# A gather of features is issued only when the third one ahead of it has landed

## What is computed

```
w_m = (efeat @ W_msg + b_msg).reshape(E, in_f, -1)
w_a = (efeat @ W_attn + b_attn).reshape(E, in_f, -1)
h_src = feat[src][:, :, None]
e1 = w_m * h_src
e2 = w_a * h_src
seg_max = jax.ops.segment_max(e2, dst, num_segments=N)
ex = jnp.exp(e2 - seg_max[dst])
denom = jax.ops.segment_sum(ex, dst, num_segments=N)
attn = ex / denom[dst]
ft = jax.ops.segment_sum(e1 * attn, dst, num_segments=N)
return ft.sum(axis=1)
...
x = _layernorm(x + _L0_gnn_ref(x, edge_attr_16, L0_gnn_W_msg, L0_gnn_b_msg, L0_gnn_W_attn, L0_gnn_b_attn, src, dst), axis=-1)
x = _layernorm(x + _L1_gnn_ref(x, edge_index, edge_attr_16), axis=-1)
```

## Time and profile before

| | |
|---|---|
| median of 3 runs | 2309.12 us (2309.01 to 2309.82) |
| the profiled execution | 2309.43 us |
| its span in the trace | 2307.6 us |
| POOL busy | 1682.1 us (73%), 1748 instructions |
| DVE busy | 1867.7 us (81%), 2922 instructions |
| PE busy | 2005.4 us (87%), 6784 instructions |
| ACT busy | 1306.8 us (57%), 1241 instructions |
| mean share of the 16 DMA engines by the gathers' queue | 9.3% |

### The profile page before, as it was taken

The page is one execution under the profiler, slowest core; times in us unless marked ns, Lnnn a source line. Parts: engine busy times, 40 slices in busy tenths (PEclk is TensorE's granted clock), DMA queues, the critical chain, the costliest instruction groups (busy, mean ns, idle before and its releaser), DMA issues.

```text
span 2307.6 us, 21909 instructions
## 1 busy us (share of the span) xinstructions
PE 2005.4 (87%) x6784; PEld 911.8 (40%) x6784; DVE 1867.7 (81%) x2922; ACT 1306.8 (57%) x1241; POOL 1682.1 (73%) x1748
## 2 busy tenths in 40 slices
PE   2548889998999998899989898899989898998886
PEld 0313334443444444444444443344444443444432
DVE  5557777987888988888987887798878887888886
ACT  6425545655566556665655755565556565565552
POOL 5777777777777777777777777777777777777740
PEclk8758999999999999999999999999999999999998
DMA  6100011001100001000100110101001010110110
GB/s 232 55 13 13 13 15 19 7 13 18 13 12 13 13 13 17 12 12 13 17 12 12 17 12 12 17 12 16 12 12 16 12 15 12 15 15 11 14 27 9
DMA packets 60072, 46.93 MB, mean 20 GB/s; under 512 B 28526, under 2 KB 55679, under 8 KB 59436
## 3 DMA queue, kind: packets, MB, share of 16 engines
q0 software_dynamic: 57776, 29.87, 9.3%
q1 hardware_dynamic: 2172, 15.58, 1.9%
HBM read 44.01 MB, written 1.23 MB: 20 GB/s over the span
## 4 chain that ended last, share of the span: by engine, by line
PE 36%; POOL 30%; issue 14%; DVE 14%; DMA 2%; ACT 2%; POOLq 0%; DVEq 0%; SPq 0%; ACTq 0%
POOL AR L624 29%; PE PX L1048 28%; PE PW L1034 7%; DVE AR L1348 7%; DVE AR L1361 3%; PE PTB L1023 2%; DVE AR L1378 1%; DMA AR<-in_xt,AR 1%; POOL AR L642 1%; DVE AR L1365 1%; POOL y_d L657 1%; DMA AR<-in_dst,QI 1%; ACT PX L881 0%; DVE AR L1379 0%; DMA AR<-in_es,AR 0%
## 5 line engine op out<-in xcount | busy, mean ns | idle before, releaser
L624 POOL DMA_INDIRECT AR<-in_xt,AR x1628 | 1572.2, 966 | 501.0 <-issue 486.6
L1048 PE MATMUL PX<-AR,CS 128*128 128x512 f32 x3304 | 1583.4, 604 | 6.8 <-ACT AR L825 6.6
L1348 DVE CUSTOM_DVE_ANT_1 AR<-PW,AR 128x1024 f32<-128x1024 f32 x826 | 987.7, 1220 | 183.0 <-PE PW L1034 127.6
L1048 PEld LDWEIGHTS PX<-AR,CS 128*128 128x128 f32 x3304 | 633.7, 193 | 586.5 <-issue 462.6
L1034 PE MATMUL PW<-WS,LT 100*128 100x512 bf16 x1652 | 514.8, 398 | 204.0 <-DVE AR L1348 203.0
L1361 DVE TENSOR_TENSOR AR<-AR,PX 128x1024 f32<-128x1024 f32 (+1 forms) x448 | 508.2, 1134 | 74.3 <-ACT PX L881 47.7
L819 ACT ACTIVATE LT<-PTB 100x1024 bf16<-100x1024 bf16 (+1 forms) x224 | 214.3, 957 | 529.8 <-PE PTB L1023 529.8
L883 ACT ACTIVATE AR<-AR 128x2048 f32<-128x2048 f32 (+1 forms) x224 | 429.3, 1917 | 7.3
L887 ACT ACTIVATE PX<-AR 128x1024 f32<-128x1024 f32 (+1 forms) x224 | 217.2, 970 | 326.4 <-DVE AR L1361 323.6
L1034 PEld LDWEIGHTS PW<-WS,LT 100*128 100x128 bf16 x1652 | 144.9, 99 | 584.2 <-issue 290.0
L881 ACT ACTIVATE PX<-AR 128x1024 f32<-128x1024 f32 (+1 forms) x224 | 235.6, 1052 | 22.9 <-DVE AR L1361 21.3
(11 more groups left out here) (149 smaller groups left out, 481.8 us busy)
## 6 DMA issues: line engine op xcount, KB each, us to landing
AR<-in_xt,AR POOLq DMA_INDIRECT x1631, 2.3
AR<-in_ea SPq DMA_DIRECT2D x3, 3128.0 KB, 13.6
AR<-in_ea SPq DMA_DIRECT2D x1, 3120.0 KB, 10.2
AR<-in_es,AR POOLq DMA_INDIRECT x49, 3.5
y_d<-AR POOLq DMA_INDIRECT x49, 2.1
AR<-y_d SPq DMA_DIRECT2D x1, 784.0 KB, 4.6
CS<-in_cst SPq DMA_DIRECT2D x1, 442.0 KB, 5.1
AR<-in_xt SPq DMA_DIRECT2D x1, 392.0 KB, 3.1
```

Source lines behind the costliest of these rows:

```text
L624: g.indirect_dma_start(feat(h, j - j0, j - j0 + 1), None, xt, bass.IndirectOffsetOnAxis(ap=XE[:, at:at + 1], axis=0)).then_inc(hg_sem(h), 16)
L1048: i = pe.matmul(PDR, IDN, x, start=(a == 0 and j == 0), stop=(g == LAST[k] and j == n - 1))
L1348: v.tensor_tensor_reduce(em(g, j, j + 2).rearrange("p (x c) -> p x c", c=32), w, hb, 1.0, LOW, ALU.mult, ALU.max, accum_out=MXC[:, k % 2, ...
```

## The change

Three semaphores `d_h[0..2]` take the place of all those for the gathers. All 1,628 gathers are numbered in the order of issue, x = 0, 1, 2, ..., and gather x adds to `d_h[x % 3]`. From x = 3 on, its issue waits for `d_h[x % 3]` to reach 16 * (x // 3), that is for gather x - 3 to have landed. Who needs a group g waits for all three semaphores, each at the count that it has once the last gather of g and all before it have landed (`landed`). Neither the order of the instructions nor any size is changed. In the changed file the lines of POOL are 1 or 2 lower, L624 is L623 there, and DVE's L1334 is L1330.

```diff
+FLIGHT = 3
+SLOTS = [max(0, min(n, CAPS[k] - j0)) for k, j0, n, a in GRP]
+UPTO = [sum(SLOTS[:g + 1]) for g in range(NGR)]
...
-        d_h0 = [sem(f"d_h0_{a}") for a in range(LAST[0] + 1)]
-        d_hl = [sem(f"d_hl{a}") for a in range(LAST[NC - 1] - FIRST[NC - 1] + 1)]
-        d_h = [sem(f"d_h{i}") for i in range(4)]
+        d_h = [sem(f"d_h{i}") for i in range(FLIGHT)]
...
+        def landed(e, g):
+            n = UPTO[g]
+            for i in range(FLIGHT):
+                e.wait_ge(d_h[i], 16 * ((n - i + FLIGHT - 1) // FLIGHT))
...
             def gather(k, h):
-                j0, n = GRP[h][1:3]
-                for j in range(j0, min(j0 + n, CAPS[k])):
+                j0, n = GRP[h][1], SLOTS[h]
+                for j in range(j0, j0 + n):
+                    x = UPTO[h] - n + j - j0
+                    if x >= FLIGHT:
+                        g.wait_ge(d_h[x % FLIGHT], 16 * (x // FLIGHT))
                     at = xoff[k % 3] + 17 * j
                     g.indirect_dma_start(feat(h, j - j0, j - j0 + 1), None, xt,
-                                         bass.IndirectOffsetOnAxis(ap=XE[:, at:at + 1], axis=0)).then_inc(hg_sem(h), 16)
+                                         bass.IndirectOffsetOnAxis(ap=XE[:, at:at + 1], axis=0)).then_inc(d_h[x % FLIGHT], 16)
...
-                        for h in range(FIRST[k - 3], LAST[k - 3] + 1):
-                            g.wait_ge(hg_sem(h), hg_count(h))
+                        landed(g, LAST[k - 3])
...
                 def floors(lo, hi):
                     k, j0 = GRP[lo][0:2]
-                    for g in range(lo, hi):
-                        v.wait_ge(hg_sem(g), hg_count(g))
+                    landed(v, hi - 1)
```

More of the change, by code:

```diff
@@ L671, in regular @@
                 g.wait_ge(S["a_p"], 4 * MAIN + 3)
-                for h in range(FIRST[MAIN], LAST[MAIN] + 1):
-                    g.wait_ge(hg_sem(h), hg_count(h))
+                landed(g, LAST[MAIN])
                 for k in range(MAIN, NC):
@@ L1497, in general @@
                 v.wait_ge(d_xe[0], 16)
-                for h in range(SOON):
-                    v.wait_ge(hg_sem(h), hg_count(h))
+                landed(v, SOON - 1)
                 for g5 in range(10):
```

## The result

The changed kernel takes **2324.78 us** (median of 4 runs, 2323.35 to 2327.09), the kernel before on the same chip 2309.47 us (4 runs): a ratio of 1.0065 with a 95% interval of 1.0047 to 1.0082. That is slower by 15 us, where 7.5 were forecast. The direction was right; the size was half of what came, and the time lies above the range. The kernel before was timed anew beside each batch of experiments.

The account below looks back on a forecast made before the run. POOL was taken to pace the kernel at the beginning and in the second half. The start's +7.5 us, with all other terms at nothing, on 2309.1 gave 2316.6 us; the 8-in-10 range was 2311.5 to 2323.

Parts of the forecast that it names:

- What bounds the kernel: POOL, issuing a gather every 1.25 us, paces beginning and second half; its losses since 31.8 us reach the end in full.
- the signs of being wrong: Last gather moving by a different amount than the 48th, or the end moving by less than the last gather.
- The start, +7.5 us: Landings of about 7 us under SP's loads make POOL lose 6 gathers by 67.6 us, 1.25 us each.
- the rule of the Trainium skill: Tensor_tensor should not hold descriptor generation; stretch would then be the queue's, its 9 us before 70 us would go, sum -1.5.
- The wait instruction, 0: Waits added to 1,625 gathers cost nothing, hidden under the gather in front; other bound 0.01 us each, 16 us.
- "Is the wait met, in the long middle?": Landings within 3.47 us cost nothing, so no loss; other bound 47 classes by 0.25 us, 12 us.
- the slow landing: Landing time of a gather in the middle: median 2.3 us, typical slow one 3.2, worst 3.8.
- The stretch in the middle, not costed: Stretched gathers, explained for the first 90 us by DVE's two-operand instructions, stay in place; no term for the middle.
- "nothing, with a bound of -5": DVE's `floors` waiting for three semaphores costs nothing; bound -0.2 us for each of 26 waits.
- "Slower by much more": Gathers behind an edge fetch miss 3.47 us, or met waits cost: 12 to 16 us more, about 2330; chance 0.10.
- "No change": Waits are met everywhere or the start is covered, nothing is lost, time 2309 us; chance 0.13.
- "faster": DVE paces the second half; the finer wait saves 5 to 10 us over 26 waits, 2301 us; chance 0.04.

Follow-up runs that it names:

- eight in flight: The changed kernel with eight semaphores in place of three, so up to eight gathers in flight; ratio 0.9998 (0.9989 to 1.0007) against the kernel before.
- the kernel that has this part alone: The kernel before with the rule of three in flight for class 0's gathers only, later gathers without such a wait; ratio 1.0035 (1.0021 to 1.0049).
- The two sets of runs: The changed kernel, unaltered, timed in two batches against the kernel before: ratio 1.0065 (1.0047 to 1.0082), then 1.0085 (1.0071 to 1.0098).
- with 83 packets: The changed kernel with 8 more instructions (16 met waits) before each of TensorE's 826 pairs of slots; ratio 1.0106 (1.0090 to 1.0121) against the kernel before.

## Why the prediction was wrong, point by point

- **What bounds the kernel: right.** Six gathers' worth of work at the start came out at the end, and a change that loses nothing on POOL (eight in flight) costs nothing. DVE's waits for gathers in the second half are 88 us, 87 before. One of the signs of being wrong did show: the last gather moved by 19.1 us where the 48th moved by 8. The other did too, by little: the end moved by 17.5 us, 1.6 us less than the last gather.
- **The start, +7.5 us: right in its mechanism, and a little lucky in its size.** It is 8.2 in the profile, 8 us by the kernel that has this part alone. The gaps came where they were forecast, under SP's loads, and went with them. But they hold 10.2 us of waiting, not 7.5, and a loss of stretch that the forecast had at nothing takes 1.8 back, 1.4 of it before 70 us. Most of the stretch of the first 70 us stayed (7.5 of 9.0 us). There were gathers of 3.02, 2.14, 2.87 and 2.26 us with at most three in flight, so a crowded queue is not what stretches them. The forecast had set this against the rule of the Trainium skill, page "SBUF — State Buffer", section "Who interferes with whom". The entry that it cites also says that a tensor_tensor with both inputs in SBUF contends with GpSimd's reads. A gather takes its source numbers out of XE in SBUF, so by that part of the entry it could be held. The trace agrees with this part, by the gather of 2.28 us beside DVE's tensor_tensor.
- **The wait instruction, 0: right.**
- **"Is the wait met, in the long middle?": the step that failed.** I took nothing, with 12 us as the other bound. 21 of 1,612 waits from 70 us on were missed, for 6.3 us. Two terms were too small. One is the slow landing, taken at 3.2 to 3.8 us. It reaches 4.3 us, and about as much where no wait is felt (4.1 us with eight in flight), so it was most likely there before the change as well, where the profile could not show it. There the gathers shared a semaphore, so the next gather's increments filled the count while one of the 16 was missing. The other is the 0.28 us from the signal to POOL's start: at 6 of the 21 it is 0.76 to 1.68 us, which leaves as little as 3.75 - 1.68 = 2.07 us for a landing. The Trainium skill says this of two transfers on one semaphore, page "DMA: Bandwidth & Descriptors", section "Why a DMA increments its semaphore by 16 and not by 1": the count can be reached early because the later DMA's engines complete first. This case agrees: from 169 us on, the traces show 2 landings over 3.47 us before and 20 after, with the same 57 instruction packets.
- **The stretch in the middle, not costed: the second miss.** I let the stretched gathers stay where they are in time, but from 1130 us on DVE starts by the gathers' own landings, so that DVE's place beside POOL's issues is not free. It cost 4.6 us in the profile. That DVE's place beside POOL's issues makes it is likely and not shown. I gave DVE's changed waits in `floors` "nothing, with a bound of -5", since DVE idles anyway. That bound had only one sign: I priced what DVE saves and not what it does to POOL.
- **The rivals.** "Slower by much more" had the right two places in it (waits missed behind slow landings, and about 2330 us), with a chance of 0.10. Its mechanism was off: gathers behind an edge fetch were not what missed, but those with an instruction packet behind them. "No change" and "faster" fell with the gaps at the start.

The sum by the profile: 8.2 + 6.3 + 4.6 = 19.1 us at the last gather, 17.5 of them at the end of the span. The two sets of runs, at 15 and 20 us, lie around this.

## What to carry to other kernels

A limit on transfers in flight is paid by the slowest of them and not by the median, so size it by the tail, and measure that tail with one semaphore for each transfer in flight, since a shared one hides it. Add the time from the landing to the engine's start, and take its worst case too. Here three were too few, four missed no wait in the middle, and eight were free everywhere. Here DVE's `floors`, released by the landings of gathers that POOL issues, starts at nearly the same place in POOL's rhythm each time: ask of every change to such a wait not only what the waiter gains but beside which instruction of the pacing engine it now starts.

## What the runs showed of the hardware

- Behind a single 16 KB packet of TensorE's instruction queue, one of the 16 increments of an 8 KB gather comes 1.1 to 2.0 us late. With 57 such packets 18 waits for a gather were missed in this way, with 83 packets 30.
- From the landing to the start of the gather that waits for it POOL takes 0.26 us, but 0.76 to 1.68 us at certain gathers, the same ones in each profile (three of them at 1.64 to 1.68 us).
- A wait that is already met costs POOL nothing visible behind a 0.94 us gather: 1,600 of them, 0.9998 (0.9989 to 1.0007).
- A gather takes 1.05 to 1.26 us on average, up to 1.52 us, when DVE's `floors` (two operands in SBUF) starts up to 0.3 us ahead of it, and 0.96 to 0.97 us when it starts just behind.
- DVE's `floors` starts 0.22 us (median) after the landing behind several waits, be they on one semaphore or on eight, and 0.08 us after it behind those on three or four.
